# Relation aggregate of a four-layer graph kernel: messages in two float32r parts instead of three bf16 parts, counts cast by halves

## The chip, the cores and the metric

The kernel runs on one core of one Trainium2 chip. The metric is the device time of one execution in microseconds; beside it stands the time of the one execution that the hardware profiler recorded. The engines are named as in the profile: PE is the matrix engine (PEld its weight loads), DVE the vector engine, ACT the scalar engine, POOL GpSimd, SP the engine that issues the transfers.

## What is computed

Four graph layers run in a row on the same 1875 nodes and 60000 edges (`src`, `dst`, sorted by `dst`), each followed by a residual and a layer norm. The change concerns the second layer, which has two relations (edge types):

```python
def _L1_gnn_ref(feat, src, dst, rel, W_rel, b_rel, W_ih, b_ih, b_hh, W1, b1, W2, b2, W3, b3):
    S = feat[src]
    def edge_nn(x, W, b):
        h = jax.nn.relu(x @ W.T + b)
        return jax.nn.relu(h @ W.T + b)
    msgs = jnp.zeros_like(S)
    for r in range(W_rel.shape[0]):
        msgs = jnp.where((rel == r)[:, None], edge_nn(S, W_rel[r], b_rel[r]), msgs)
    agg = jax.ops.segment_sum(msgs, dst, num_segments=n_nodes)
    gates = agg @ W_ih.T + b_ih + b_hh
    ...
```

A message depends on the source node and the relation only. So the kernel computes it once per node and relation, and the sum over edges is a product with a matrix of edge counts: `agg[d] = sum over r, s of count[r][s, d] * message[r][s]`. The third layer (SAGE, two convolutions) sums over all edges in the same way, with the counts of both relations added and a division by the number of edges of each node.

## The kernel before

The nodes are 15 tiles (`NT`, also called `SH`) of 128. The counts lie in `adjacency` (`ADJ`, 128 x 2 x 28320, uint16): for a relation and a source tile `sh`, the 1888 counts (`NW`) of all destinations stand 15 elements apart. Every engine runs its own instruction list, written out by hand and tied together by semaphores; nothing is reordered by a scheduler.

The stages around the change are these.

- **Messages** (PE lines 1733 and 1758, function `messages1` on ACT, `rest` on DVE). For ten groups (two relations, five groups of three node tiles) PE computes the hidden layer into PSUM, ACT applies the ReLU, PE computes three message tiles of 128 x 256 from it. For each of the 30 message tiles ACT writes the ReLU rounded to bf16 (line 691); DVE subtracts it from the PSUM value (1285), writes that remainder as bf16 (1286) and subtracts again into a third bf16 part (1287). PE's message products of a group wait (`m_ev`) until DVE has done the messages of the group before.
- **Relation aggregate** (`aggregate(CH1, R2 * SH, 0)`, PE line 1776). Thirty count chunks, one for a relation and source tile. ACT casts each chunk of 1888 counts to f16 (line 713) into a ring of two; a cast waits until the chunk two before has been used (`chunk_used`). For each chunk PE makes 24 products of 128 x 128 by 128 x 472: three parts, two feature halves (`fo`), four column groups (`j`) of the 1888, all accumulated in the eight PSUM banks.
- **Counts per node** (DVE lines 1318 to 1321), beside the aggregate. Once ACT has cast the last chunk of relation 0, DVE adds the counts of relation 1 to those of relation 0 in place, sums the 15 source tiles into `CNTX`, waits for the end of the aggregate, and copies `CNTX` to `CNTS`.
- **Evacuation** (`agg_evac`, DVE 1314 and 1315, ACT 725): the eight banks go to `XT`, then PE starts the gates (`gates`, line 1796).
- **Weights of the rest of the layer** (SP lines 467 to 470): the loads of `WIH`, `W1s`, `W2s`, `W3s` wait for the last message (`m_ev`).

The two aggregates of the third layer use the same function with one chunk per source tile (15) and with messages in two float32r parts, `halves`: ACT writes the ReLU as float32r, DVE the remainder (1293) as float32r. There the chunk is cast to float32r too, its first 944 columns by ACT (733) and its second 944 by DVE (1378), again in a ring of two. This is the path that the change takes over for the relation aggregate.

A flag (`large`), loaded from the input's counts, selects another path with full float32 messages (`WIDE`); the rows show that the other path ran.

Names: `s["..."]` are the semaphores, `A_...` are offsets (in 4-byte words) into the one large SBUF tensor `arena`, `CW` is 472.

Of the kernel before, what the change touches and what calls it, by code (L numbers as in the profile page):

```python
# [34 lines left out]
D = 256  # L35
# [124 lines left out]
MW = 3 * D // 2  # L160
A_CNT = A_B1 + NT * MW
A_FB = A_WT - RRING * FW
assert A_FB >= A_HB + D and A_OR >= A_X + NT * D
assert A_CNT + NW <= A_CH and A_B1 + R2 * NT * MW <= A_WT and A_B1 + 12 * CN <= A_CNT
# [4 lines left out]
def build(nc, rec, x, xT, edge0, w0, a0l, a0r, cols, hrow, wrel, brow, wih, w1, w2, w3, b3, wp1, bp1, wl1, bl1, wr1, wp2, bp2, wl2, bl2, wr2,  # L169
          wt3, a3l, a3r, out):  # L170
    ctx = ExitStack()
    with ctx:
# [131 lines left out]
        MT = [AR[:, A_B1 + MW * i:A_B1 + MW * (i + 1)] for i in range(R2 * NT)]  # L304
        CNTS = ar(A_CNT, NW)

        def parts(i):
            return [MT[i].bitcast(BF16)[:, D * q:D * (q + 1)] for q in range(3)]

        HALVES = nc.alloc_sbuf_tensor_at("message_halves", [P, 2 * NT * D], F32R, offset=a_at + 4 * A_B1)  # L310
        COUNTS = nc.alloc_sbuf_tensor_at("count_chunks", [P, 2 * NW], F32R, offset=a_at + 4 * A_CH)

        def halves(i):
            return [HALVES[:, D * (2 * i + q):D * (2 * i + q + 1)] for q in range(2)]

        WIDE = [AR[:, A_B1 + D * i:A_B1 + D * (i + 1)] for i in range(R2 * NT)]

        def chunk(at, k, wide):

            if at == CH2 and not wide:  # L320
                return COUNTS[:, k * NW:(k + 1) * NW]
            if wide:
                return AR[:, at[1] + k * NW:at[1] + (k + 1) * NW]
            return AR[:, at[0] + k * NW // 2:at[0] + (k + 1) * NW // 2].bitcast(F16)

        REM = ar(A_REM, D)
        CH1, CH2 = (A_XT + 2 * NP - NW, A_B1 + R2 * NT * D), (A_CH, A_CH)
# [9 lines left out]
        WIH = ar(A_WT + 1024, 2, 3 * D)  # L337
        W1s, W2s, W3s = ar(A_WT + 2560, 2, P), ar(A_WT + 2816, P), ar(A_WT + 2944, D)
# [16 lines left out]
            var_ready std_ready ln_done xt_mm xt_eva xt_evd h_mm h_ev m_mm m_ev chunk_ready chunk_half chunk_used agg_eva  # L355
# [14 lines left out]
        def offsets(engine, step, n, most, table=OFF):  # L370
# [4 lines left out]
                skip_runtime_bounds_check_because="window and tile numbers of the walk stay in range for any sorted edges")[1]  # L375

# [12 lines left out]
        def _(sp):  # L389
# [75 lines left out]
            sp.wait_ge(s["m_ev"], 3 * R2 * NC)  # L465
# [106 lines left out]
        def _(act):  # L572
# [115 lines left out]
            def message(n, bank, wide, exact=False):  # L688

                dst = WIDE[n % (R2 * NT)] if wide else halves(n)[0] if exact else parts(n % (R2 * NT))[0]  # L690
                a.activation(dst, PS[bank][:, 0:D], ACT.Relu).then_inc(s["hi_ready"], 1)

            def messages1(wide):
# [14 lines left out]
                act.wait_ge(s["m_mm"], 3 * R2 * NC)  # L708
                for c in range(R2 * SH):
# [3 lines left out]
                    a.activation(chunk(CH1, c % 2, wide), ADJ[:, r, :].rearrange("p (n s) -> p n s", s=SH)[:, :, sh],  # L713
                                 ACT.Copy).then_inc(s["chunk_ready"], 1)

            with act.If(large < 1):
                messages1(False)
            with act.If(large >= 1):
# [1218 lines left out]
```

## Time and profile before

| what | us |
|---|---|
| median of 3 runs | 1783.98 (1782.76 to 1784.89) |
| the profiled execution | 1781.72 |
| its span, first to last instruction | 1780.0 |
| PE / DVE / ACT / POOL busy | 1422.1 / 1154.4 / 749.8 / 546.0 |
| messages and relation aggregate, from the first hidden product to the first gate product | 1138.2 to 1364.5 |
| in it the relation aggregate's products | 1214.56 to 1360.75 |

The rows quoted further on come from this one profiled execution. Times in them are from the start of its span. In the groups of instructions, "busy, mean ns" are the time in which the group was busy and the mean length of one instruction (matmuls overlap, so the mean times the count is more than the busy time); "idle before" is the time in which the engine did nothing just before such an instruction, with what ended the wait.

### The profile page before, as it was taken

How to read it: one execution, taken by the hardware profiler on the slowest of the kernel's cores; microseconds unless marked ns; L12 is line 12 of the kernel's file. 1: busy time of each engine (PE TensorE's matmuls, PEld its weight loads, DVE VectorE, ACT ScalarE, POOL GpSimd, SP SyncE). 2: the span in 40 equal slices, each digit the busy share in tenths (PEclk: the TensorE clock that was granted, in tenths of full speed). 3: DMA queues.
4: the chain of work that ended last, by engine and by line, in shares of the span. 5: the costliest groups of instructions: out<-in, count | busy, mean ns of one | idle time of the engine just before them, and what ended most of it. 6: DMA issues, size and time to landing. Idle time of an engine off the chain costs nothing.

```text
span 1780.0 us, 21845 instructions
## 1 busy us (share of the span) xinstructions
PE 1422.1 (80%) x5158; PEld 758.0 (43%) x5158; DVE 1154.4 (65%) x2990; ACT 749.8 (42%) x1243; POOL 546.0 (31%) x517
## 2 busy tenths in 40 slices
PE   5897987777777777773499999798999989989840
PEld 2454643411111111112277777454445447758630
DVE  6323543399999999999989988751180443543727
ACT  1333443477777777772000000236774435416022
POOL 0103777777777777771000000000000000000023
PEclk9997555755555555555599999898999979999965
DMA  4534666655555555552098888000000010000023
GB/s 163 167 133 154 210 210 213 211 185 187 185 186 185 179 187 184 186 185 85 25 322 275 266 273 256 1 1 26 1 1 2 0 36 0 2 12 1 1 62 74
DMA packets 84507, 223.90 MB, mean 126 GB/s; under 512 B 18456, under 2 KB 27588, under 8 KB 83908
## 3 DMA queue, kind: packets, MB, share of 16 engines
q1 hardware_dynamic: 60452, 158.01, 25.4%
q0 software_dynamic: 23968, 64.77, 14.0%
q8 instruction: 51, 0.84, 0.2%
q14 instruction: 36, 0.29, 0.1%
HBM read 140.09 MB, written 82.63 MB: 125 GB/s over the span
## 4 chain that ended last, share of the span: by engine, by line
PE 43%; DVE 20%; issue 14%; POOL 6%; DMA 2%; ACT 2%; DVEq 2%; SPq 0%; POOLq 0%
PE bank L1776 14%; PE bank L1711 13%; POOL arena L557 6%; DVE arena L1095 4%; DVE arena L1096 3%; DVE adjacency L1102 3%; PE bank L1796 2%; DVE arena L1137 2%; PE bank L1833 2%; PE bank L1758 2%; PE bank L1733 2%; DMA arena<-feat_table,arena 1%; PE bank L1865 1%; DVEq L372 1%; PE bank L1862 1%
## 5 line engine op out<-in xcount | busy, mean ns | idle before, releaser
L557 POOL DMA_INDIRECT arena<-feat_table,arena x469 | 508.8, 1085 | 240.1 <-issue 227.9
L1650 PE MATMUL bank<-arena 128*128 128x480 f16 x586 | 337.0, 576 | 122.0 <-DVE arena L1096 116.0
L639 ACT ACTIVATE arena<-bank 128x480 uint16<-128x480 f32 x586 | 333.4, 572 | 118.1 <-PE bank L1650 111.6
L565 POOL DMA_INDIRECT arena<-al_table,edge_ends x15 | 14.8, 985 | 917.4 <-DMA al_table<-arena 913.2
L1102 DVE TENSOR_TENSOR adjacency<-adjacency,arena 128x480 uint16 x586 | 235.5, 402 | 9.9 <-DVE arena L1115 6.2
L1650 PEld LDWEIGHTS bank<-arena 128*128 128x128 f16 x586 | 61.0, 104 | 398.3 <-DVE arena L1096 312.0
L1711 PE MATMUL bank<-arena 128*128 x966 | 229.6, 392 | 0.9 <-issue 0.3
L1096 DVE TENSOR_SCALAR arena<-iota,arena 128x480 f16<-128x480 f16 x586 | 199.2, 340 | 0.0
L1711 PEld LDWEIGHTS bank<-arena 128*128 128x128 f32 x966 | 173.4, 190 | 57.3 <-issue 36.4
L1193 DVE TENSOR_TENSOR arena<-arena 128x1024 f32<-128x1024 f32 x118 | 140.1, 1214 | 16.4 <-DMA arena<-edge_rows 14.5
L1776 PE MATMUL bank<-arena 128*128 128x472 f16 x720 | 146.2, 367 | 3.9 <-ACT arena L713 3.9
L1095 DVE TENSOR_SCALAR arena<-iota,arena 128x128 f16<-128x128 f16 x586 | 145.9, 249 | 1.3 <-ACT adjacency L603 1.3
L713 ACT ACTIVATE arena<-adjacency 128x1888 f16<-128x1888 uint16 x30 | 109.0, 3638 | 34.9 <-PE bank L1776 34.9
L1570 PE MATMUL bank<-arena 128*128 128x512 f32 x240 | 108.8, 608 | 5.7 <-ACT arena L588 3.0
L1776 PE MATMUL bank<-count_chunks,message_halves 128*128 128x472 f32 x480 | 103.4, 377 | 2.1 <-DVE message_halves L1293 2.1
L1776 PEld LDWEIGHTS bank<-arena 128*128 128x128 bf16 x720 | 71.1, 99 | 79.3 <-ACT arena L713 4.7
L671 ACT ACT_TABLE_LOAD x2 | 2.6, 1283 | 240.0 <-DVE ln_mean_var L1239 240.0
L1776 PEld LDWEIGHTS bank<-count_chunks,message_halves 128*128 128x128 f32 x480 | 90.0, 188 | 15.5 <-issue 2.9
L1613 PE MATMUL bank<-arena 128*128 x588 | 75.7, 189 | 17.1 <-DVE arena L1052 11.3
L733 ACT ACTIVATE count_chunks<-adjacency 128x944 fp32r<-128x944 uint16 (+1 forms) x30 | 69.9, 2335 | 39.8 <-PE bank L1776 39.8
L1613 PEld LDWEIGHTS bank<-arena 128*128 128x128 f16 x588 | 60.1, 105 | 48.4 <-issue 35.0
L1200 DVE TENSOR_TENSOR arena<-iota,arena 128x1024 f32<-128x1024 f16 (+1 forms) x61 | 73.8, 1210 | 7.0 <-PE bank L1711 6.9
(294 smaller groups left out, 1598.0 us busy)
## 6 DMA issues: line engine op xcount, KB each, us to landing
arena<-edge_rows SPq DMA_DIRECT2D x117, 520.0 KB, 4.7
edge_rows<-arena SPq DMA_DIRECT2D x67, 520.0 KB, 2.9
edge_rows<-arena SPq DMA_DIRECT2D x67, 390.0 KB, 2.6
feat_table<-arena SPq DMA_DIRECT2D x60, 260.0 KB, 2.1
arena<-feat_table,arena POOLq DMA_INDIRECT x469
arena<-in_w SPq DMA_DIRECT2D x1, 2048.0 KB, 9.7
arena<-in_xT SPq DMA_DIRECT2D x1, 1920.0 KB, 18.0
arena<-in_x SPq DMA_DIRECT2D x1, 1792.0 KB
```

What stands on the lines that cost most here:

```text
L557: g.indirect_dma_start(out=PLACE[k][:, t - lo, :], out_offset=None, in_=feat_t, in_offset=bass.IndirectOffsetOnAxis(ap=IE[:, t:t + 1], axi ...
L639: a.activation(EV[st % AS].rearrange("p r k -> p (r k)"), PS[4 + st % 4][:, 0:R2 * KW], ACT.Copy)\
L713: a.activation(chunk(CH1, c % 2, wide), ADJ[:, r, :].rearrange("p (n s) -> p n s", s=SH)[:, :, sh], ACT.Copy).then_inc(s["chunk_ready"], 1)
L1095: v.tensor_scalar(OHS[st % AS], iota128[:, :], lo, None, ALU.is_equal)
L1096: v.tensor_scalar(OHK[st % AS], iota480[:, :], key, None, ALU.is_equal).then_inc(s["a_oh"], 1)
L1102: v.tensor_tensor(dst, dst, EV[st % AS], ALU.add).then_inc(s["a_add"], 1)
L1193: v.tensor_tensor(rows, rows, al, ALU.mult).then_inc(s["r_wgt"], 1)
L1570: ins = mm(PS[c][:, :], XT0[:, k, P * t:P * (t + 1)], W0[:, k, 512 * c:512 * (c + 1)], start=(k == 0), stop=(k == 1))
L1613: ins = mm(PS[4 + g % 2][:, 3 * H * k:3 * H * (k + 1)], KO[g % 3][:, lo:lo + P], ERW[:, bass.ds(offs[k], 3 * H)], start=True, stop=True)
L1650: mm(PS[4 + st % 4][:, 0:R2 * KW], OHS[st % AS], OHK[st % AS], start=True, stop=True).then_inc(s["a_mm"], 1)
L1711: mm(BANKS[:, bass.ds(out_at, D)], OHR[:, (st // RG) % ORING, P * (st % RG):P * (st % RG + 1)], FBf[:, bass.ds(places[st % RK] >> 12, D)], ...
L1776: ins = mm(PS[4 * fo + j][:, 0:CW], m[:, P * fo:P * (fo + 1)], ch[:, CW * j:CW * (j + 1)], start=(c == 0 and q == 0), stop=(c == n - 1 and ...
```

## The change

The relation aggregate gets a function of its own, `aggregate_relations`.

- The message is two float32r parts: ACT writes the ReLU as float32r, DVE one remainder (`low_half` in place of `rest`). The 30 messages take 30 x 512 words in place of 30 x 384 and lie in four places (`halves1`): 22 from `A_M1`, one each at `A_M22` and `A_M23`, and the last six where `XT` is (the transposed input, read for the last time by the hidden products).
- A chunk is cast to float32r in halves of 944 counts (`HW`), 60 in all, in a ring of three (`RING1`, `NRING`). Half `h` waits until half `h - 3` has been used (`half_free`). `cast_on_dve` says who casts: of relation 0 ACT the even and DVE the odd halves; of relation 1 ACT all of the first 11 source tiles, and DVE the odd halves of the last four (halves 53, 55, 57, 59).
- PE makes 8 products per half: two parts, two feature halves, two column groups; 480 in all in place of 720.
- The counts per node: DVE adds the relations once its and ACT's halves of relation 0 are cast, then waits until 19 chunks have been used, because the sum now goes straight to `CNTS`, which lies at `A_CH` among the messages; only after it come DVE's halves of relation 1. The copy from `CNTX` is gone.
- The weights of the rest of the layer move to `A_WIH`, where the first messages lie, and are loaded once 14 chunks have been used.
- The third layer's aggregates keep their work under new names.

```diff
+HW = NW // 2
+NRING, SPLIT1 = 3, SH - 4
...
+A_CNT = A_CH
+A_WIH = A_M1 + 9 * 2 * D
+def cast_on_dve(h):
+    r, sh = h // (2 * SH), h // 2 % SH
+    return h % 2 == 1 and (r == 0 or sh >= SPLIT1)
...
+        def half_free(engine, h):
+            past = h - NRING
+            if past >= 0 and past % 2:
+                engine.wait_ge(s["chunk_used"], past // 2 + 1)
+            elif past >= 0:
+                engine.wait_ge(s["first_half_used"], past // 2 + 1)
...
-            sp.wait_ge(s["m_ev"], 3 * R2 * NC)
+            sp.wait_ge(s["chunk_used"], 14)
...
+            with act.If(large < 1):
+                messages1(False)
+                for h in range(2 * R2 * SH):
+                    if not cast_on_dve(h):
+                        half_free(act, h)
+                        a.activation(RING1[h % NRING], count_half(h), ACT.Copy).then_inc(s["cast_act"], 1)
...
-                link(v.scalar_tensor_tensor(REM, PS[bank][:, 0:D], 0.0, hi, ALU.max, ALU.subtract))
-                link(v.tensor_copy(mid, REM))
-                v.tensor_tensor(lo, REM, mid, ALU.subtract).then_inc(done, 1)
...
             with dve.If(large < 1):
                 for n in range(R2 * NT):
-                    rest(n, n, 4 + n % 3, s["m_ev"], n)
+                    low_half(n, halves1(n), 4 + n % 3, s["m_ev"])
+                for h in range(1, 2 * SH, 2):
+                    half_free(dve, h)
+                    v.tensor_copy(RING1[h % NRING], count_half(h)).then_inc(s["cast_dve"], 1)
+                dve.wait_ge(s["cast_act"], casts_to(2 * SH - 1, False))
+                dve.wait_ge(s["cast_dve"], casts_to(2 * SH - 1, True))
...
-            dve.wait_ge(s["chunk_ready"], SH)
             link(v.tensor_tensor(ADJ[:, 0, :], ADJ[:, 0, :], ADJ[:, 1, :], ALU.add))
-            link(v.tensor_reduce(CNTX, ADJ[:, 0, :].rearrange("p (n s) -> p n s", s=SH), AX.X, ALU.add))
-            dve.wait_ge(s["chunk_used"], R2 * SH)
-            v.tensor_copy(CNTS, CNTX).then_inc(s["cnt_red"], 1)
-            dve.wait_ge(s["cnt_red"], 1)
+            both = ADJ[:, 0, :].rearrange("p (n s) -> p n s", s=SH)
+            with dve.If(large < 1):
+                dve.wait_ge(s["chunk_used"], 19)
+                v.tensor_reduce(CNTS, both, AX.X, ALU.add).then_inc(s["cnt_red"], 2)
+                for h in range(2 * SH, 2 * R2 * SH):
+                    if cast_on_dve(h):
+                        half_free(dve, h)
+                        v.tensor_copy(RING1[h % NRING], count_half(h)).then_inc(s["cast_dve"], 1)
...
+            def add_products(m, ch, j0, start, stop):
+                for fo in range(2):
+                    for j in range(ch.shape[1] // CW):
+                        ins = mm(PS[4 * fo + j0 + j][:, 0:CW], m[:, P * fo:P * (fo + 1)], ch[:, CW * j:CW * (j + 1)], start=start, stop=stop)
+                return ins
...
+                    for h in range(2 * R2 * SH):
+                        c, part = h // 2, h % 2
+                        if cast_on_dve(h):
+                            pe.wait_ge(s["cast_dve"], casts_to(h, True))
+                        else:
+                            pe.wait_ge(s["cast_act"], casts_to(h, False))
+                        hi, lo = halves1(c)
+                        add_products(hi, RING1[h % NRING], 2 * part, c == 0, False)
+                        add_products(lo, RING1[h % NRING], 2 * part, False, c == R2 * SH - 1)\
+                            .then_inc(s["chunk_used"] if part else s["first_half_used"], 1)
```

Two places show how the instructions now stand. DVE before, from the last message to the evacuation of the aggregate (`[waits ...]` names the semaphores an instruction waits for; line numbers are those of the kernel before):

```order
L1285 SCALAR_TENSOR_TENSOR arena<-bank,arena 128x256 [waits m_ev,hi_ready]
L1286 CAST arena<-arena 128x256 [waits dve_link]
L1287 TENSOR_TENSOR arena<-arena 128x256 [waits dve_link]
...
L1318 TENSOR_TENSOR adjacency<-adjacency 128x28320 [waits chunk_ready]
L1319 TENSOR_REDUCE arena<-adjacency 128x1888 [waits dve_link]
L1321 COPY arena<-arena 128x1888 [waits chunk_used,dve_link]
L1314 COPY arena<-bank 128x472 [waits chunk_used,cnt_red]
```

DVE of the change at the same place (line numbers of the changed kernel; `count_half_0` and `count_halves_1_2` are the three places of the ring, `last_messages` the last six messages; the number behind a name is the buffer's):

```order
L1327 SCALAR_TENSOR_TENSOR last_messages_54<-bank,last_messages_54 128x256 [waits hi_ready] x6
L1339 CAST count_halves_1_2_56<-adjacency 128x944
L1339 CAST count_half_0_55<-adjacency 128x944 [waits first_half_used]
L1339 CAST count_halves_1_2_56<-adjacency 128x944 [waits first_half_used] x2
...
L1334 UNCONDITIONAL_BRANCH [waits cast_dve,cast_act]
...
L1354 TENSOR_TENSOR adjacency<-adjacency 128x28320
L1356 COMPARE_AND_BRANCH [waits dve_link]
L1358 TENSOR_REDUCE arena<-adjacency 128x1888 [waits chunk_used]
L1362 CAST count_halves_1_2_56<-adjacency 128x944 [waits first_half_used] x2
L1362 CAST count_half_0_55<-adjacency 128x944 [waits first_half_used]
L1362 CAST count_halves_1_2_56<-adjacency 128x944 [waits first_half_used]
```

Fifteen casts now stand ahead of the addition, and four stand behind the sum over source tiles (halves 53, 55, 57, 59), which itself waits for a used chunk; the copy is gone.

ACT before, from the last messages on:

```order
L691 ACTIVATE arena<-bank 128x256 [waits m_mm] x6
L713 ACTIVATE arena<-adjacency 128x1888 [waits m_mm]
L713 ACTIVATE arena<-adjacency 128x1888
L713 ACTIVATE arena<-adjacency 128x1888 [waits chunk_used] x28
```

ACT of the change at the same place, with the change from relation 0 to relation 1 at the end of the piece:

```order
L731 ACTIVATE last_messages_54<-bank 128x256 [waits m_mm] x6
L755 ACTIVATE count_half_0_55<-adjacency 128x944 [waits m_mm]
L755 ACTIVATE count_halves_1_2_56<-adjacency 128x944
L755 ACTIVATE count_halves_1_2_56<-adjacency 128x944 [waits chunk_used]
...
L755 ACTIVATE count_half_0_55<-adjacency 128x944 [waits chunk_used]
L755 ACTIVATE count_halves_1_2_56<-adjacency 128x944 [waits first_half_used]
L755 ACTIVATE count_halves_1_2_56<-adjacency 128x944 [waits chunk_used]
L755 ACTIVATE count_half_0_55<-adjacency 128x944 [waits first_half_used]
```

Thirty whole chunks have become 41 halves: every other half of relation 0, then one half after the other.

## Rows read from the trace of the kernel before

**Rows 1.** The page's first lines: span, and PE's busy time.
```profile
span 1780.0 us, 21845 instructions
...
PE 1422.1 (80%) x5158; PEld 758.0 (43%) x5158; DVE 1154.4 (65%) x2990; ACT 749.8 (42%) x1243; POOL 546.0 (31%) x517
```
**Rows 2.** The chain that ended last, 1100 to 1780: start us, us, what.
```profile
1151.70 2.58 PE bank L1733 x8
...
1211.04 3.48 ACT arena L713
1214.56 146.19 PE bank L1776 x720
1360.85 1.16 DVE arena L1321
1362.03 2.32 DVE arena L1314 x4
1364.52 10.73 PE bank L1796 x24
...
1378.43 7.85 PE bank L1796 x24
```
**Rows 3.** Groups of instructions by line and shape, 1136 to 1378.
```profile
L1776 PEld LDWEIGHTS bank<-arena 128*128 128x128 bf16 x720 | 71.1, 99 | 79.3 <-ACT arena L713 4.7 <-issue 3.3
```
**Rows 4.** The same view, 1447 to 1535: the third layer's first aggregate.
```profile
L1776 PE MATMUL bank<-count_chunks,message_halves 128*128 128x472 f32 x240 | 51.7, 377 | 1.0 <-DVE message_halves L1293 1.0
L1776 PEld LDWEIGHTS bank<-count_chunks,message_halves 128*128 128x128 f32 x240 | 45.0, 188 | 7.8 <-issue 1.4
L733 ACT ACTIVATE count_chunks<-adjacency 128x944 fp32r<-128x944 uint16 x13 | 27.8, 2135 | 19.9 <-PE bank L1776 19.9
L1378 DVE CAST count_chunks<-adjacency 128x944 fp32r<-128x944 uint16 x13 | 15.1, 1158 | 31.2 <-PE bank L1776 31.2
```
**Rows 5.** Timeline, start of the aggregate: start us, us, instruction [idle before <-releaser].
```profile
1203.39 0.42 DVE L1285 SCALAR_TENSOR_TENSOR arena<-bank,arena 128x256 f32<-128x256 f32 x1
1204.18 0.42 DVE L1287 TENSOR_TENSOR arena<-arena 128x256 bf16<-128x256 f32 x1
1204.75 0.26 PE L1756 MATMUL bank<-arena,ones 3*128 3x256 bf16 x1 [1.91 <-DVE arena L1287]
1204.94 1.13 PE L1758 MATMUL bank<-arena 128*128 128x256 f32 x4
1208.54 2.08 PE L1758 MATMUL bank<-arena 128*128 128x256 f32 x4
1210.93 7.05 ACT L713 ACTIVATE arena<-adjacency 128x1888 f16<-128x1888 uint16 x2
```
**Rows 6.** Stretches: PE, PEld, DVE, ACT, POOL busy (instructions), PEclk, DMA share, GB/s.
```profile
1203.00:1206.00 3.00, 1.25 (x5) 0.77 (x5) 1.43 (x4) 0.27 (x1) 0.00 (x0) 1.00 0.00 0
1208.00:1210.50 2.50, 2.50 (x6) 1.27 (x5) 1.15 (x3) 0.38 (x1) 0.00 (x0) 0.50 0.00 0
1217.00:1219.90 2.90, 2.90 (x9) 1.11 (x8) 0.00 (x0) 0.99 (x1) 0.00 (x0) 0.50 0.01 5
1219.90:1225.00 5.10, 5.10 (x27) 2.50 (x26) 0.00 (x0) 2.84 (x1) 0.00 (x0) 1.00 0.00 0
1364.50:1370.00 5.50, 5.48 (x9) 3.08 (x10) 0.00 (x0) 0.58 (x1) 0.00 (x0) 0.50 0.00 0
1478.00:1482.00 4.00, 3.29 (x15) 2.93 (x16) 0.42 (x1) 0.08 (x1) 0.00 (x0) 1.00 0.00 0
```
**Rows 7.** Timeline, ACT in the relation aggregate: beside nothing, beside DVE's sum.
```profile
1255.62 3.64 ACT L713 ACTIVATE arena<-adjacency 128x1888 f16<-128x1888 uint16 x1 [1.15 <-PE bank L1776]
1260.40 3.63 ACT L713 ACTIVATE arena<-adjacency 128x1888 f16<-128x1888 uint16 x1 [1.14 <-PE bank L1776]
...
1303.42 3.64 ACT L713 ACTIVATE arena<-adjacency 128x1888 f16<-128x1888 uint16 x1 [1.12 <-PE bank L1776]
```
**Rows 8.** Timeline, ACT in the third layer's aggregate: two casts with their waits.
```profile
1489.29 2.13 ACT L733 ACTIVATE count_chunks<-adjacency 128x944 fp32r<-128x944 uint16 x1 [1.31 <-PE bank L1776]
...
1496.14 2.13 ACT L733 ACTIVATE count_chunks<-adjacency 128x944 fp32r<-128x944 uint16 x1 [1.26 <-PE bank L1776]
```
**Rows 9.** Timeline, DVE in the relation aggregate: addition and sum.
```profile
1283.18 14.91 DVE L1318 TENSOR_TENSOR adjacency<-adjacency 128x28320 uint16<-128x28320 uint16 x1 [70.90 <-ACT arena L713]
1298.13 29.65 DVE L1319 TENSOR_REDUCE arena<-adjacency 128x1888 f32<-128x28320 uint16 x1
```
**Rows 10.** Timeline, SP: the first of the four weight loads.
```profile
1212.31 0.38 SPq L467 DMA_DIRECT2D arena<-in_wih  x1
```

More of the change, by code:

```diff
@@ L712, in messages1 @@
                         act.wait_ge(s["chunk_used"], c - 1)
[L713 to L718, printed above, removed]
-                messages1(True)
+                    a.activation(chunk(CH1, c % 2, True), ADJ[:, r, :].rearrange("p (n s) -> p n s", s=SH)[:, :, sh],
+                                 ACT.Copy).then_inc(s["cast_act"], 1)
             def agg_evac(dst, total):
@@ L1307, in _ @@
                     no_rest(n, s["m_ev"])
[L1308 removed]
+                dve.wait_ge(s["cast_act"], SH)
             def agg_evac(dst, total):
@@ L1761, in _ @@
             pe.wait_ge(s["m_ev"], 3 * R2 * NC)
-            def aggregate(at, n, first):
-                def products(wide):
-                    for c in range(n):
-                        pe.wait_ge(s["chunk_ready"], first + c + 1)
-                        if at == CH2 and c >= 2:
-                            pe.wait_ge(s["chunk_half"], (first // SH - R2) * (SH - 2) + c - 1)
-                        ch = chunk(at, c % 2, wide)
-                        ms = [WIDE[c]] if wide else halves(c) if at == CH2 else parts(c)
-                        for q, m in enumerate(ms):
-                            for fo in range(2):
-                                for j in range(4):
-                                    ins = mm(PS[4 * fo + j][:, 0:CW], m[:, P * fo:P * (fo + 1)], ch[:, CW * j:CW * (j + 1)],
-                                             start=(c == 0 and q == 0), stop=(c == n - 1 and q == len(ms) - 1))
+            def add_products(m, ch, j0, start, stop):
[3 more added lines that the diff above has]
+                return ins
@@ new lines, in aggregate, with chunks @@
+            def aggregate(u):
+                def chunks(wide):
+                    for c in range(SH):
+                        pe.wait_ge(s["chunk_ready"], SH * u + c + 1)
+                        if c >= 2:
+                            pe.wait_ge(s["chunk_half"], u * (SH - 2) + c - 1)
+                        ch = chunk(CH2, c % 2, wide)
+                        if wide:
+                            ins = add_products(WIDE[c], ch, 0, c == 0, c == SH - 1)
+                        else:
+                            hi, lo = halves(c)
+                            add_products(hi, ch, 0, c == 0, False)
+                            ins = add_products(lo, ch, 0, False, c == SH - 1)
```

83 lines of the change are left out of this document (51 added, 32 removed).

## The prediction

> **What bounds the kernel now.** I read the page first [rows 1]: PE is busy 80% of the span, but that is an average over stages. The chain that ended last [rows 2] shows the stage of the change by itself: 720 products of line 1776 follow one another for 146.19 us with nothing else between them, so the relation aggregate is bound by PE. Ahead of it the chain runs over ACT's first cast, behind it over DVE's copy (1.16 us) and its evacuation (2.32 us). Whatever shortens PE's work here shortens the kernel until another engine is later than PE. So I need PE's pace, the pace of the casts, and DVE's long instructions.
>
> **PE's pace.** ACT's casts in the steady part start 4.78 us apart [rows 7], one per 24 products: 199.2 ns each. 720 x 0.1992 = 143.4 us. The other 2.8 us of the 146.19 are the clock: from 1214.56 to 1219.9 the granted clock was 0.50, the 1.2 GHz level, then 1.00 [rows 6]; half of 5.3 us is 2.7 us lost. The new products are those of the third layer's aggregate, same shape and type. There ACT's casts start 3.425 us apart over 16 products (6.85 us for two chunks, [rows 8]): 214 ns each, 1.715 us for a half of 8. 60 halves: 102.9 us. Were PE never to wait, the stage would shrink by 40 us.
>
> The float32r weights load slower: 188 ns on average against 99 ns for bf16 [rows 3, 4]. The 15 ns by which a product is slower may come from that. The Trainium skill ("TensorE: Matmul & The Clock Gate", Weight-path perf modes) says that fast weight load is on only where the type isn't FP32; the 188 against 99 agrees. It speaks against the change; by it alone, with the longer load fully in the open (89 ns x 480), the sum would be some 43 us longer, but the third layer's aggregate already runs at 214 ns with these loads, so I keep 214.
>
> **The casts.** A half on ACT took 2.13 us, beside DVE's cast that starts at the same instant, a half on DVE 1.16 us [rows 4]. Alone, a half on ACT is not in the trace. From below: half of a whole chunk, 3.63 / 2 = 1.81 us [rows 7]; from above 2.13. I take 1.9, nearer to the whole chunk, which also ran alone. Two casts in a row took 7.05 us [rows 5] against 2 x 3.63, so one follows the other some 0.15 us before the length says: a pace of 1.75 (1.65 to 2.0).
>
> Let t = 0 be PE's first product, at full clock. In relation 0, half h may be cast from the end of half h-3 and is needed when h-1 ends, 3.43 us later. ACT needs 0.2 us (the semaphore) + 2.1 + 0.1 = 2.4, DVE 1.5: no wait. In relation 1 ACT casts 22 halves in a row, from h = 30. That one is ready at 28 x 1.715 + 0.2 + 2.0 = 50.2 and needed at 51.5. At 1.75 ACT loses 0.035 a half on PE: never late. At 2.0 it is late by 5 us at h = 52.
>
> **DVE is the one that is late.** Its last cast of relation 0 (half 29) starts when half 26 ends, 46.5, and ends at 47.7. The addition takes 14.9 us [rows 9]: 62.7. The sum waits for 19 used chunks, 38 halves: 38 x 1.715 + 0.2 = 65.4; the addition is covered by 2.7 us. The sum takes 29.65 us [rows 9]: 95.05. Half 53 stands behind it in DVE's queue: + 1.16 + 0.1 = 96.3. PE wants it at 53 x 1.715 = 90.9. **PE stands still for about 5 us at half 53**, or for 1 us if ACT's pace is 2.0, with the same end. Then 7 halves remain, 12.0 us: 108.3. The other halves of DVE and ACT fit in the ring (3.43 us against 1.5 and 2.4).
>
> The clock: I keep the 2.7 us at the start: 111.0. The stall is a second occasion. After the 3.8 us without products before 1364.5 the granted clock was 0.50 until 1370 [rows 6], also 5.5 us, 2.7 lost; after the gap of 1.0 before the third layer's aggregate it stayed 1.00 [rows 4, 6]. A stall of 5 us resembles the first, so I add 2.7: **113.7 us for the aggregate, 32.5 less than 146.2**.
>
> **The edges of the stage.**
> - PE's first product waited for a whole chunk: last message product until 1210.62, cast from 1210.93, product at 1214.56 [rows 2, 5]. A half is enough now (1.9 + 0.1): 1212.9, **1.6 us** less. Half 1 on DVE (one short instruction for the last message, then 1.16) is ready then too.
> - DVE's work on a message falls from three instructions to one. PE sees it once, at the last group, where nothing else covers: it waited 1.91 us [rows 5] for DVE, whose last message ran from 1203.39 to 1204.60. Now it ends after the first instruction, 1203.81: **0.8 us** less. The other nine groups are covered by the next hidden products (2.58 us, [rows 2]).
> - The copy to CNTS goes from the chain: 1.16 us, **1.2** with its semaphore [rows 2]. The evacuation (2.32) stays.
> - The weight loads: SP issued them from 1212.31 [rows 10]; now after 14 chunks (28 halves, 48 us into the stage), with some 60 us until the gates. Nothing stands behind them on SP but the bias rows that wait for the aggregate's end as before. Cost nothing; were the cover gone, the gates would wait for the landing. More instructions and waits on ACT (41 for 30): inside the 1.75. Storage moves cost nothing.
>
> **Sum.** 32.5 + 1.6 + 0.8 + 1.2 = 36.1 us less. On the profiled execution: 1781.7 - 36.1 = 1745.6. The median of the runs is 2.3 us above that execution, so 1784.0 - 36.1 = 1747.9; I say **1748**. From no change I could tell 0.2%, 3.6 us.
>
> **Unknown terms.** Below: no clock price at the stall (-2.7), none at the start (-2.7), and the fall of the clock at 1206 [rows 6] avoided with the shorter gap there (two message tiles at 2.08 in place of 1.13, [rows 5], -1.9). Above: DVE's sum beside an ACT that never pauses (before, it paused 1.14 of 4.78 us; up to +1), or the clock low for all 12 us after the stall (+9.3).
>
> **Rivals.**
> - *The stall doesn't cost clock* (27%). For: the chunk before ran at full speed; if ACT's pace is near 2.0, the waiting is spread over many halves and the gap at 53 is 1 us. 1748 - 2.7 = 1745. The Trainium skill (same page, The HAM clock gate) says that the level follows recent activity and that the array is slowed after idleness; which gap suffices only the rows above bear on: 1.0 us no, 3.8 yes.
> - *ACT is the bound of relation 1* (6%). If its pace passes 2.03 (from 50.2 + 22p + 1.7 > 96.3), half 53 waits for half 52 and each 0.1 us adds 2.2 us. At 2.2 this is +4: 1752. Against: no row of ACT shows a half above 2.2.
> - *Clock low longer after the stall* (8%): up to 1757.
> - *A change of weights costs* (4%). A weight tile now serves two products, before four. If each change cost the whole load, 4 more changes per chunk, 30 x 4 x 0.188 = 22.6 us on PE: 125.5 + 2.7 = 128.2, with the stall absorbed: 1784 - 18.0 - 3.6 = 1762. Against: there is one load per product already [rows 4].
> - *The loads come into the open* (3%), the other side. If every product waited for its own load, 197 + 188 = 385 ns, the stage would be 480 x 0.385 + 2.7 = 187.5 us: 1784 + 41.3 - 3.6 = 1822. It becomes slower than before from (143.4 + 3.6) / 480 = 306 ns a product. Against: 214 ns in rows of the same shape; the waits at every half instead of every chunk are all that could break the overlap.
> - *Not what it says*: if the flag chose the full float32 path, nothing of this would run; the rows of before show the bf16 and f16 shapes on the same input. Under 1%.
>
> **How the numbers follow.** Forecast 50%, no clock price 27, clock low longer 8, ACT the bound 6, change of weights 4, loads in the open 3, the rest 2 (some gain lost elsewhere, about no change). The range reaches down to 1741 (the three clock terms) and up to 1757 (low clock to the end): it leaves out the last three cases and a piece of the others. Faster 0.95, same 0.02, slower 0.03.
>
> **What would show it.** 480 products of 8 per half, 214 ns apart; ACT's halves of relation 1 at 1.8 to 2.0 us; the sum of 29.7 us starting 68 us after PE's first product (65.4 + 2.7); one idle of PE of 1 to 5 us in front of half 53, released by DVE's cast; granted clock 0.50 behind it; no copy between aggregate and evacuation; PE idle 2.3 us before the first product. Wrong if products are farther apart than 220 ns, if PE waits for ACT's halves in relation 0, or if the sum isn't followed by a stall.

## The result and the profile after

The changed kernel takes 1737.16 us (median of 4 runs, 1733.44 to 1739.31) against 1783.37 us before (4 runs, 1781.29 to 1784.89): ratio 0.9745, 95% interval 0.9718 to 0.9772, or 46 us less. I had said 1748, with 1741 to 1757. The direction and the place are right; the gain is 10 us larger than forecast, and the measured time lies 4 us below the range.

The profiled execution of the changed kernel took 1739.31 us, its span 1737.6. First its page (head and PE's busy time, which answer to [rows 1]):

```profile
span 1737.6 us, 21308 instructions
...
PE 1378.4 (79%) x4918; PEld 774.2 (45%) x4918; DVE 1153.8 (66%) x2948; ACT 722.7 (42%) x1254; POOL 545.3 (31%) x517
```

The chain that ended last in the stage (start us, us, what), which answers to [rows 2]:

```profile
1209.95 1.81 ACT count_half L755
1211.81 59.66 PE bank L1813 x272
...
1275.49 3.97 PE bank L1813 x16
...
1279.56 29.65 DVE arena L1358
1309.21 0.93 DVE count_halves L1362
...
1310.18 12.29 PE bank L1813 x56
...
1322.49 2.32 DVE arena L1351 x4
...
1324.99 7.98 PE bank L1866 x24
```

DVE's sum (line 1358) and the cast of half 53 behind it (line 1362) stand in the chain between two runs of products, as forecast, and 56 products, seven halves, are left behind it; the copy ahead of the evacuation is gone. The first 24 gate products took 7.98 us where they took 10.73 before. Timelines: PE at the last message tiles, at the start of the aggregate and at half 53; then DVE from its addition to the casts of halves 53 and 55.

```profile
1205.67 0.26 PE L1802 MATMUL bank<-arena,ones 3*128 3x256 bf16 x1 [1.02 <-DVE last_messages L1327]
1211.81 3.37 PE L1813 MATMUL bank<-count_half,first_messages 128*128 128x472 f32 x8 [2.27 <-ACT count_half L755]
...
1310.18 1.98 PE L1813 MATMUL bank<-count_halves,last_messages 128*128 128x472 f32 x8 [1.64 <-DVE count_halves L1362]
```
```profile
1261.17 14.91 DVE L1354 TENSOR_TENSOR adjacency<-adjacency 128x28320 uint16<-128x28320 uint16 x1 [0.52 <-DVE count_halves L1339]
1279.56 29.65 DVE L1358 TENSOR_REDUCE arena<-adjacency 128x1888 f32<-128x28320 uint16 x1 [3.47 <-PE bank L1813]
1309.13 2.01 DVE L1362 CAST count_halves<-adjacency 128x944 fp32r<-128x944 uint16 x2
```

The stretches that answer to [rows 6] (columns as there; the granted clock is the number ahead of the last two) are, in this order, the last messages, the start of the aggregate, the products behind the stall, and the gates.

```profile
1205.50:1209.50 4.00, 3.83 (x15) 2.30 (x15) 0.87 (x3) 0.77 (x2) 0.00 (x0) 1.00 0.00 0
1211.80:1215.00 3.20, 3.19 (x8) 2.74 (x9) 0.00 (x0) 1.78 (x1) 0.00 (x0) 0.52 0.00 0
...
1310.20:1313.00 2.80, 2.80 (x13) 2.48 (x14) 0.94 (x1) 0.80 (x1) 0.00 (x0) 1.00 0.00 0
...
1325.00:1330.00 5.00, 5.00 (x16) 3.01 (x17) 0.00 (x0) 2.47 (x4) 0.00 (x0) 1.00 0.01 3
```

Only one of the four is low, the start of the aggregate, for 3.2 us instead of 5.3. Before, the last messages and the gates were low too.

From such timelines I made one sheet for every profile: the time from the first hidden product to the last message product, then each gap and block of products. The stage runs from the first hidden product to the second group of gate products; in it, behind the first 24 gate products, 30 products of one column stand that take 3.2 us in every profile and have no column. A block of gates is counted to the start of the next product, so 10.73 and 7.98 us above are 10.6 and 7.8 here. "Ahead" and "behind" are what lies before and after the stage. All in us.

| kernel | messages | gap | aggregate | gap | 24 gate products | stage | ahead | behind |
|---|---|---|---|---|---|---|---|---|
| before | 72.6 | 3.9 | 146.2 | 3.8 | 10.6 | 240.3 | 1138.0 | 401.7 |
| change | 69.7 | 2.3 | 110.6 | 2.5 | 7.8 | 196.2 | 1139.8 | 401.6 |

The stage gives 44.1 us: 2.9 + 1.7 + 35.5 + 1.2 + 2.7. The rest of the program gives back 1.7, nearly all of it ahead of the stage, where nothing was changed.

### The profile page after: what moved, and what is told of

It is laid out like the page before. It is cut to its first block, busy times and chain, and to the rows that moved or that the text cites. A ratio compares the mean times of both kernels' runs of the same rounds, so it can differ in the third digit from the quotient of the medians.

```text
span 1737.6 us, 21308 instructions
## 1 busy us (share of the span) xinstructions
PE 1378.4 (79%) x4918; PEld 774.2 (45%) x4918; DVE 1153.8 (66%) x2948; ACT 722.7 (42%) x1254; POOL 545.3 (31%) x517
## 4 chain that ended last, share of the span: by engine, by line
PE 43%; DVE 22%; issue 10%; POOL 6%; ACT 5%; DMA 3%; DVEq 2%; SPq 0%; POOLq 0%
PE bank L1757 13%; PE bank L1813 11%; POOL arena L597 6%; DVE arena L1139 4%; ACT arena L679 3%; DVE arena L1140 3%; PE bank L1696 3%; DVE adjacency L1146 3%; PE bank L1866 2%; PE bank L1903 2%; DVE arena L1181 2%; PE bank L1804 2%; DMA arena<-feat_table,arena 2%; DVE arena L1358 2%; PE bank L1779 2%
## 5 line engine op out<-in xcount | busy, mean ns | idle before, releaser
L1146 DVE TENSOR_TENSOR adjacency<-adjacency,arena 128x480 uint16 x586 | 252.0, 430 | 10.2 <-DVE arena L1159 6.2
L1140 DVE TENSOR_SCALAR arena<-iota,arena 128x480 f16<-128x480 f16 x586 | 216.2, 369 | 0.0
L1757 PEld LDWEIGHTS bank<-arena 128*128 128x128 f32 x966 | 175.6, 191 | 54.9 <-issue 32.9
L1139 DVE TENSOR_SCALAR arena<-iota,arena 128x128 f16<-128x128 f16 x586 | 162.9, 278 | 0.9 <-ACT adjacency L643 0.9
L628 ACT ACTIVATE arena<-bank 128x512 f32<-128x512 f32 x60 | 35.8, 597 | 99.9 <-PE bank L1616 96.2
L1645 PE MATMUL bank<-adjacency,ident 128*128 128x512 f16 x128 | 66.2, 616 | 12.6 <-ACT arena L655 9.7
L1616 PEld LDWEIGHTS bank<-arena 128*128 128x128 f32 x240 | 46.8, 199 | 62.0 <-issue 54.8
```

The costliest lines, as they stand in the source:

```text
L1139: v.tensor_scalar(OHS[st % AS], iota128[:, :], lo, None, ALU.is_equal)
L1140: v.tensor_scalar(OHK[st % AS], iota480[:, :], key, None, ALU.is_equal).then_inc(s["a_oh"], 1)
L1146: v.tensor_tensor(dst, dst, EV[st % AS], ALU.add).then_inc(s["a_add"], 1)
L1616: ins = mm(PS[c][:, :], XT0[:, k, P * t:P * (t + 1)], W0[:, k, 512 * c:512 * (c + 1)], start=(k == 0), stop=(k == 1))
L1757: mm(BANKS[:, bass.ds(out_at, D)], OHR[:, (st // RG) % ORING, P * (st % RG):P * (st % RG + 1)], FBf[:, bass.ds(places[st % RK] >> 12, D)], ...
```

## The experiments

Fifteen more runs were made: twelve edited kernels, the changed kernel twice more and the kernel before once more. The sheet has a profile of each, with the gap in front of half 53, the time from the first gate product to the third layer's first product ("gates"), and the median time with the number of runs in brackets. Executions of the changed kernel lie up to 6 us apart, so the time of a single run settles nothing smaller; the readings below rest on the blocks.

| kernel | messages | aggregate | gap at 53 | gap | 24 gate products | stage | gates | behind | time |
|---|---|---|---|---|---|---|---|---|---|
| before | 72.6 | 146.2 | | 3.8 | 10.6 | 240.3 | 90.9 | 401.7 | 1783.37 (4) |
| e_before_again | 71.2 | 145.9 | | 3.8 | 10.4 | 238.4 | 91.0 | 397.9 | 1776.91 (1) |
| change | 69.7 | 110.6 | 1.6 | 2.5 | 7.8 | 196.2 | 86.4 | 401.6 | 1737.16 (4) |
| e_again | 69.8 | 110.7 | 1.7 | 2.5 | 7.8 | 196.4 | 85.7 | 397.9 | 1735.51 (5) |
| e_after_third | 69.8 | 110.6 | 1.5 | 2.5 | 7.8 | 196.2 | 88.5 | 397.3 | 1734.50 (1) |
| e_copy_back | 69.8 | 110.7 | 1.5 | 3.7 | 9.5 | 199.1 | 98.8 | 408.8 | 1748.31 (1) |
| e_three_ops | 73.1 | 110.9 | 1.7 | 2.5 | 7.8 | 199.8 | 86.5 | 401.5 | 1741.08 (1) |
| e_longer_stall | 69.7 | 115.2 | 4.5 | 2.5 | 7.8 | 200.7 | 91.6 | 399.9 | 1741.67 (1) |
| e_no_sum | 69.8 | 108.8 | 0 | 2.5 | 9.5 | 196.1 | 90.3 | 401.1 | 1739.37 (1) |
| e_no_sum_split | 69.7 | 106.0 | 0 | 2.5 | 9.5 | 193.2 | 92.0 | 404.6 | 1740.08 (1) |
| e_all_act | 68.8 | 109.2 | 0 | 2.5 | 9.3 | 195.4 | 93.7 | 403.6 | 1737.65 (1) |
| e_ring_two | 68.6 | 123.8 | 0 | 2.5 | 7.8 | 208.2 | 90.4 | 404.5 | 1752.63 (1) |
| e_sum_early | 69.7 | 108.8 | 0 | 2.5 | 9.5 | 196.0 | 90.3 | 397.7 | 1735.13 (4) |
| e_sum_in_pieces | 69.8 | 105.9 | 0 | 2.5 | 9.5 | 193.2 | 87.9 | 401.4 | 1735.82 (5) |
| e_early_gates | 69.7 | 110.6 | 1.7 | 0.8 | 7.8 | 194.4 | 91.0 | 399.2 | 1735.24 (4) |
| e_pieces_early_gates | 69.9 | 106.1 | 0 | 0.8 | 7.8 | 190.0 | 86.3 | 401.2 | 1734.70 (5) |
| e_pieces_gap | 69.4 | 106.1 | 1.4 | 2.6 | 9.4 | 193.0 | 93.9 | 404.2 | 1735.19 (1) |

**The changed kernel and the kernel before, again** (e_again, e_after_third, e_before_again; no edit).

> The changed kernel once more, unchanged, to see how far single executions scatter. Theory A (the stage gives a fixed gain, the rest scatters): the stage from the first hidden product to the second group of gate products takes 196.1 us again within 0.5, the aggregate 110.7, and times lie between 1733 and 1740 with a gain of 42 to 48 us over the kernel before; what varies lies ahead of 1140 us. Theory B (the clock falls in the stage in some executions, not in others): the aggregate or the gates differ by 1 to 3 us from the first profile.

> The changed kernel a third time. Theory A (a matter of the moment): aggregate 110.7, and gates at another length than the 86.4 and 85.8 us of the first two profiles, up to 99. Theory B (the shorter gap in front of the gates keeps the clock up): 85.5 to 86.5 us again, first 24 gate products in 7.8.

> The kernel before, once more, to see whether the time behind the aggregate varies from one execution to the next. Theory A (the granted clock in the gates is a matter of the moment): aggregate 146.2 again, but 86 to 99 us from the first gate product to the third layer's first product, where the first profile had 90.9. Theory B (it is fixed by the kernel): 90.9 within 0.5.

e_again: 1735.51 us (5 runs, 1733.08 to 1738.33), before beside it 1783.08 (9 runs, 1775.42 to 1788.81), ratio 0.974, interval 0.9714 to 0.9766. The stage is the same in three profiles of the changed kernel within 0.2 us: theory A on the stage. But what varies does not lie ahead of 1140 us, as theory A had it: the three profiles differ by 1.4 us there and by 4.3 us behind the stage (397.3 to 401.6). e_after_third is between its theories: the first 24 gate products took 7.8 us again, as B had it, and all gates 88.5 us after 86.4 and 85.7, as A had it. The kernel before repeats its gates (90.9, 91.0), which is theory B of e_before_again, while its stage moved by 1.9 us. The clock did that: in the second profile it rose sooner at the first hidden products (1.0 us less for the first eight), the last messages lost 0.4 us less and the aggregate 0.3. So a part of what the clock costs belongs to the kernel and a part to the execution.

**The copy put back.**

> The changed kernel with a copy of 1888 elements on the vector engine put back between the aggregate and its evacuation, as before. Theory A (the evacuation's gap had cost clock): PE's gap in front of the gates grows from 2.5 to 3.7 us and the first 24 gate products take 10.7 us in place of 8.0 at a granted clock of 0.50 in their first 5 us; together 3.9 us. Theory B (the copy cost only itself): gap 3.7 us, products 8.0 us; together 1.2 us.

```diff
+            dve.wait_ge(s["chunk_used"], R2 * SH)
+            link(v.tensor_copy(AR[:, A_B1:A_B1 + NW], CNTS))
             agg_evac(XT, R2 * SH)
```

The copied counts are not used. The gap grew by 1.2 us as said, the first 24 gate products went from 7.8 to 9.5 us, and the clock was low in a part of them:

```profile
1325.00:1329.00 4.00, 3.95 (x9) 2.22 (x10) 0.00 (x0) 0.58 (x1) 0.00 (x0) 0.68 0.02 4
1329.00:1334.70 5.70, 5.70 (x20) 3.40 (x18) 0.00 (x0) 2.33 (x4) 0.00 (x0) 0.93 0.00 0
```

Together 2.9 us: theory A with 1.7 in place of 2.7 us of clock. The clock fell in four later groups of gates too, each time behind two waits of 0.67 us that left it up in the three profiles of the changed kernel. All gates took 98.8 us against 86.4, which no theory had, and this one execution 1748.31 us. Whether the copy or the execution did that, one profile can't tell.

**Three instructions a message again.**

> The changed kernel with two more vector instructions for each of the 30 messages (their results are not used), so that a message takes three instructions again. Theory A (the 1.9 us gap at the last group pulled the clock down): the gap grows from 1.0 to 1.9 us, the granted clock falls at the last messages (the last two tiles at 2.0 us in place of 1.1), and the first products of the aggregate stay low for longer than 3.2 us; together 0.9 + 1.9 + about 1.2 = 4 us. Theory B (the gap cost only itself): 0.9 us. The nine other groups cost nothing in both.

```diff
-                    low_half(n, halves1(n), 4 + n % 3, s["m_ev"])
...
+                    link(v.scalar_tensor_tensor(lo, PS[4 + n % 3][:, 0:D], 0.0, hi, ALU.max, ALU.subtract))
+                    link(v.tensor_copy(REM.bitcast(BF16)[:, 0:D], PS[4 + n % 3][:, 0:D]))
+                    v.tensor_tensor(REM.bitcast(BF16)[:, D:2 * D], PS[4 + n % 3][:, 0:D], REM.bitcast(BF16)[:, 0:D], ALU.subtract).then_inc(s["m_ev"], 1)
...
```

```profile
1205.16 0.26 PE L1808 MATMUL bank<-arena,ones 3*128 3x256 bf16 x1 [2.22 <-DVE arena L1340]
...
1206.73 2.07 PE L1810 MATMUL bank<-arena 128*128 128x256 f32 x4
...
1209.06 2.08 PE L1810 MATMUL bank<-arena 128*128 128x256 f32 x4
```

The gap became 2.2 us, 0.3 more than before (the second of the three instructions reads PSUM here and took 0.42 us, before 0.29), and the last two tiles took 2.07 and 2.08 us where the changed kernel has 1.13: messages 3.4 us longer, 1.2 by the gap and 2.2 by the clock. Theory A for the messages; of the 1.2 us that it had for the start of the aggregate only 0.2 came.

**A longer stall.**

> The changed kernel with a sum over 2640 elements (2.8 us, result not used) on the vector engine in front of its cast of half 53. PE's gap there should grow from 1.6 to about 4.4 us. Theory A (a gap of about 4 us lowers the clock): granted clock 0.50 behind it for 3 to 5.5 us, the aggregate takes 110.7 + 2.8 + 1.5 to 2.7 = 115 to 116.2 us. Theory B (after a long stretch of dense products the clock stays): 113.5 us, granted clock 1.00 throughout.

```diff
+                        if h == 53:
+                            v.tensor_reduce(REM[:, 0:176], both[:, 0:176, :], AX.X, ALU.add)
                         v.tensor_copy(RING1[h % NRING], count_half(h)).then_inc(s["cast_dve"], 1)
```

```profile
1312.63 2.90 PE L1815 MATMUL bank<-count_halves,last_messages 128*128 128x472 f32 x8 [4.46 <-DVE count_halves L1364]
```
```profile
1312.60:1316.60 4.00, 3.97 (x12) 3.39 (x13) 0.96 (x1) 1.03 (x1) 0.00 (x0) 0.60 0.00 0
```

115.2 us: 2.8 for the longer gap and 1.7 for the clock, theory A at its lower end. So a stall of 4.5 us does lower the clock here; the stall of 1.6 us that the change has does not.

**What bounds the aggregate: sum left out, casts moved, ring shortened.**

> The changed kernel without the sum over source tiles: the counts per node are set to 1 in its place, so the third layer's mean is left out. Theory A (DVE is late only by its sum, ACT's pace does the rest): the gap in front of half 53 goes (1.6 us), the aggregate takes 109.0 us, and ACT's halves of relation 1 still start 1.94 us apart. Theory B (the sum also slows ACT's casts beside it): ACT's pace falls to 1.8 us and the aggregate takes 106 to 107 us.

> The same without the sum, and DVE casts the odd halves of the last ten source tiles of relation 1 in place of the last four. Theory A (ACT's pace of 1.94 us against PE's 1.71 costs the rest): the aggregate takes 104 to 105 us (60 halves at 1.711 = 102.7, 1.5 for the low clock at the start, under 1 for ACT's first halves of relation 1). Theory B (something in PE itself, the semaphore wait at every half or the weight loads): products beyond 1.75 us a half, 107 us or more.

> The changed kernel with all halves of relation 1 on ACT. Theory A (ACT's pace bounds relation 1, DVE's four halves hardly help because they come late): no gap at half 53, PE 1.94 us a half to the end (1.9 once the sum is over); half 53 starts at 98.2 us instead of 98.4 us after the first product and the seven halves left take 7 x 1.94 = 13.6 in place of 12.1: the aggregate takes 110 to 112 us. Theory B (DVE's halves are needed): 114 us or more.

> The changed kernel with a ring of two halves in place of three. Theory (a half may then be cast only from the end of the half two before, 1.71 us ahead of its use): in relation 0 a pair of halves takes 0.2 + 2.05 + 0.1 + 1.71 = 4.1 us in place of 3.42, 10 us more over 15 pairs; in relation 1 about 2.03 us a half in place of 1.94, 1 to 2 us more: the aggregate takes 121 to 123 us. Rival (PE's order of loads and waits hides it, or casts overlap more than the rows say): under 114 us.

```diff
-                v.tensor_reduce(CNTS, both, AX.X, ALU.add).then_inc(s["cnt_red"], 2)
+                v.memset(CNTS, 1.0).then_inc(s["cnt_red"], 2)
```
```diff
-NRING, SPLIT1 = 3, SH - 4
+NRING, SPLIT1 = 3, SH - 10
+NRING, SPLIT1 = 3, SH
+NRING, SPLIT1 = 2, SH - 4
```

The first edit is that of the two kernels without the sum: all counts per node are 1 in them, so the third layer's mean is left out. Of the second, the first new line goes with it in e_no_sum_split, the second is e_all_act and the third e_ring_two, each alone.

Without the sum the aggregate takes 108.8 us (109.0 expected) and ACT's pace doesn't change:

```profile
1281.90 4.10 ACT L755 ACTIVATE count_halves<-adjacency 128x944 fp32r<-128x944 uint16 x2
1285.77 2.14 ACT L755 ACTIVATE count_half<-adjacency 128x944 fp32r<-128x944 uint16 x1
1287.68 4.09 ACT L755 ACTIVATE count_halves<-adjacency 128x944 fp32r<-128x944 uint16 x2
```

Three halves in 5.78 us, 1.93 each, as beside the sum: theory A. With DVE helping from half 41 on it takes 106.0, 1 us above what I had allowed: ACT is alone for the first eleven halves of relation 1, and the halves 33 to 41 still start 1.94 us apart. All halves on ACT: 109.2, under the 110 to 112 expected; but in this execution the start of the aggregate ran at full clock, worth 1.5 us, and with that it is 110.7, the changed kernel's own time. So DVE's four halves as placed seem to gain nothing, as far as one profile with a correction shows. The ring of two costs 13 us (15 with the same correction for its start), a little above the 121 to 123 us expected: in relation 0 PE waits 0.4 us at every second half, in relation 1 the halves start 2.08 us apart, so the third place is needed.

**Two versions with a shorter aggregate.**

> The changed kernel with CNTS two message places lower, so that DVE's sum waits for 17 used chunks in place of 19. Theory A (DVE's chain makes half 53 late): the sum starts when the addition ends, 64.3 us after PE's first product in place of 67.8, half 53 is ready before PE wants it, the gap of 1.6 us goes and the aggregate takes 109.0 us, as without any sum (108.75). Theory B (ACT's pace would be the bound by more than the gap): under 0.5 us gained.

> A version meant to beat both kernels: CNTS as in the early sum; DVE takes half 39 and all odd halves from 47 on in place of 53 on, and its sum runs in nine pieces, 944 nodes behind half 39 and 118 (the last 236) behind each later half. Theory A (DVE's one long instruction and ACT's pace are what is left above PE's own 102.7 + 1.5): the aggregate takes 105 to 106.5 us, without a gap above 0.5 us. Theory B (the pieces delay DVE's halves, each now behind 1.9 us of sum, as soon as PE catches up): 108 us or more with gaps at odd halves. The time: 1736 less 4 to 6 us, within the scatter of the gates' clock.

```diff
-A_CNT = A_CH
+A_CNT = A_WIH + 2176
...
-                dve.wait_ge(s["chunk_used"], 19)
+                dve.wait_ge(s["chunk_used"], 17)
```
```diff
-    return h % 2 == 1 and (r == 0 or sh >= SPLIT1)
+    return h % 2 == 1 and (r == 0 or sh >= SPLIT1 or h == FIRST1)
...
+                def sum_nodes(n):
+                    ins = v.tensor_reduce(CNTS[:, done[0]:done[0] + n], both[:, done[0]:done[0] + n, :], AX.X, ALU.add)
...
                         v.tensor_copy(RING1[h % NRING], count_half(h)).then_inc(s["cast_dve"], 1)
+                        if h == FIRST1:
+                            dve.wait_ge(s["chunk_used"], 17)
+                        sum_nodes(8 * PIECE if h == FIRST1 else 2 * PIECE if h == 2 * R2 * SH - 1 else PIECE)
```

Both aggregates came out as theory A had them, 108.8 and 105.9 us. The second has `FIRST1` 39, `SPLIT1` SH - 7 and `PIECE` 118, and three things at once: the early sum (1.9 us by e_sum_early), the sum in pieces, and four more halves on DVE; the two last share the other 2.8 us and weren't tried apart. And yet the stages are 196.0 and 193.2, where 194.3 and 191.5 were due: the first 24 gate products went from 7.8 to 9.5 us, with this at their start in the second:

```profile
1319.70:1323.70 4.00, 3.95 (x7) 2.21 (x8) 0.00 (x0) 1.37 (x2) 0.00 (x0) 0.57 0.02 4
```

The medians, 1735.13 (4 runs) and 1735.82 us (5 runs), ratios 0.9743 (0.971 to 0.9775) and 0.9748 (0.9721 to 0.9775), can't be told from the changed kernel's.

**The gap in front of the gates.** Every variant without a wait in relation 1 of the aggregate had the slower gates (e_no_sum, e_no_sum_split, e_all_act and these two), so I shortened the gap, and put the stall back.

> The changed kernel; PE starts the gates once the first bank of each half is evacuated, and takes each further bank when it is free, in place of waiting for all eight. The gap in front of the gates should fall from 2.5 to 0.9 us. Theory A (the gap lowers the clock, or just doesn't): first 24 gate products in 7.8 us as in the three profiles of the changed kernel; stage 196.2 - 1.6 = 194.6 us. Theory B (the clock depends on more than the gap): 9.5 us, stage 196.3.

> The sum in pieces with the early gates. The aggregate takes 105.9 us again, the gap 0.9 us. Theory A (in a kernel without a stall in the aggregate it is the gap of 2.5 us that lowers the clock): first 24 gate products in 7.8 in place of 9.5 us; stage 193.2 - 1.6 - 1.7 = 189.9 us, 6 us less than the changed kernel, its time 1729 to 1732 with the scatter of the rest. Theory B (where the clock falls is a matter of the moment): 9.5 us, stage 191.6.

> The sum in pieces with 3.8 us of unused sum in front of DVE's half 53, so that PE stands still there for about 1.8 us as the changed kernel does. Theory A (the short stall some 12 us ahead of the gap is why the changed kernel's gates ran at full clock): first 24 gate products in 7.8 us in place of 9.5, so that the stall pays for itself: aggregate 107.7, stage 193.3 us. Theory B (chance, or a matter of when the aggregate ends): 9.5 us, stage 195.0.

```diff
-                    v.tensor_copy(dst[:, 0, CW * j:CW * (j + 1)], PS[j][:, 0:CW])
+                    v.tensor_copy(dst[:, 0, CW * j:CW * (j + 1)], PS[j][:, 0:CW]).then_inc(s["m_ev"], 1)
...
-            pe.wait_ge(s["agg_evd"], 1)
-            pe.wait_ge(s["agg_eva"], 4)
...
+                    elif j < 4:
+                        pe.wait_ge(s["m_ev"], 3 * R2 * NC + j + 1)
+                    if c == 0:
+                        pe.wait_ge(s["agg_eva"], max(1, j - 3))
```

The full waits now stand behind the first group of gates. The gap fell to 0.8 us, and with the sum in pieces the gates returned to 7.8 us:

```profile
1316.00:1320.00 4.00, 3.81 (x12) 2.38 (x13) 1.85 (x6) 3.71 (x7) 0.00 (x0) 1.00 0.03 7
```

Its stage of 190.0 us is the shortest, 6.2 us under the change (189.9 expected). With the changed kernel's own aggregate the early gates gave 1.8 us in the stage; all gates took 91.0 us there, 4.6 more than in the change's first profile, so the stage's gain didn't reach the end.

e_pieces_gap has the pieces, the full waits ahead of the gates, and 3.8 us of unused sum in front of half 53:

```diff
                         half_free(dve, h)
+                        if h == 53:
+                            v.tensor_reduce(REM[:, 0:236], both[:, 0:236, :], AX.X, ALU.add)
```

PE stood still for 1.4 us there, and the gates stayed at 9.4 us: theory B, the stall didn't pay for itself in this one profile. Its aggregate, 106.1, again started at full clock; with the 1.5 us it is 107.6, as expected.

Times: e_early_gates 1735.24 us (4 runs), ratio 0.9732 (0.9708 to 0.9756); e_pieces_early_gates 1734.70 us (5 runs, 1730.15 to 1736.35), ratio 0.9719 (0.97 to 0.9737). The last is the lowest ratio of all, but its interval overlaps the changed kernel's. The 6 us of the stage are shown in the trace, a shorter total isn't.

## Why the prediction was wrong, step by step

The step that failed is the price of the clock. I added 2.7 us for a fall behind the stall, which didn't come, and I left the low clock as it was behind the three waits that the change shortens, where it shrank or went: 1.2 us at the start, 2.0 at the last messages, 2.7 in the gates. The rest of the sum holds within 1 us.

- **PE's pace** (214 ns): right. The halves start 1.71 us apart in relation 0 and 1.72 at the end, about 102.7 us for 60. The weight loads are 188 ns on average again (197 for the products that ran partly at the low clock), in the open nowhere. The two rivals on weight loads are out; the third layer's aggregate was the right place to read the price.
- **ACT's half** (1.9 us, pace 1.75): mis-sized. It took 2.0 to 2.3 us, also without a DVE cast beside it; only the first two took 1.90 us (PE idle) and 1.93 (PE's first products at the low clock). The pace was 2.0 us beside the addition and 1.93 after: at the upper end of my 1.65 to 2.0. PE lost some 4.5 us by it in short waits until half 52, and 1.6 us at once at half 53. (For a pace of 2.0 my own terms give 0.4 us there, not the 1 us that I wrote: half 52 ends at 95.9, half 53 is cast at 96.3.)
- **ACT is the bound** (rival, 6%): it didn't come, but it was close. With DVE's sum out of the way the aggregate takes 108.8 us, so DVE's end lay only 1.9 us behind ACT's. Of what is left above PE's own 102.7 and the clock's 1.5 us, ACT's pace is the larger part, and the forecast doesn't have it.
- **DVE is late at half 53**: right, and by luck so close. The sum started 67.75 us after the first product (68.1 said), took 29.65, and PE waited for the cast behind it. e_no_sum and e_sum_early took this wait away: 1.9 us. Two errors cancel in the 67.75: the clock at the start cost 1.2 us less, and ACT made PE late before the 19th chunk was used, with halves 33 to 38 starting 1.97 us apart in place of 1.71, 1.3 us in all. So the end does depend on ACT's pace, by the wait for 19 chunks, which I had denied.
- **The clock at the stall** (+2.7): wrong, and this was the choice between forecast and first rival (27%). I compared the stall of 5 us with the gap of 3.8. With ACT at 2.0 the stall was 1.6, and the rival's reason, waiting spread over many halves, was the one that came. e_longer_stall shows that the term exists, 1.7 us, from a stall of 4.5 us.
- **The clock at the start** (2.7 kept): 1.5 measured, since the low stretch was 3.2 us long.
- **The clock at the last messages**: named only as a bound (-1.9); it came in full, 2.0 us, and e_three_ops, one profile, brings it back. The shorter gap was in my own sum, and with it a reason to expect no fall; I should have taken it into the forecast.
- **The clock in the gates**: missing. The gap there fell from 3.8 to 2.5 us by the copy that I did count, and the 2.7 us of low clock behind it [rows 6], which I quoted for another purpose, went too. e_copy_back returns 1.7 of them. But the shorter gap alone doesn't explain it: six other kernels lost 1.5 to 1.7 us behind the same gap. Why the change's gates ran at full clock stays open.
- **Edges**: 1.6, 0.8 and 1.2 us forecast, 1.7, 0.9 and 1.2 measured. The weight loads from memory cost nothing.

Of the stage's 44.1 us I had 36.1: the missing 8.0 are 2.7 (stall), 1.2 (start), 2.0 (messages), 2.7 (gates), and 0.2 at the edges, less 0.8 by which the sum over source tiles, and with it the rest of the aggregate, came later than I had it (the 1.3 us above, less 0.5 by PE's slightly faster pace and a shorter semaphore). That puts the profiled execution at 1745.6 - 8.0 = 1737.6, and it took 1739.3, the rest of the program being 1.7 longer. The other 4.4 us between 1748 and 1737 are my step from one execution to the median: the profile of before lay 2.3 us below its median, that of the change 2.1 above. The program scatters by 6 us with the change and by 13 us before (1775.4 to 1788.8), so a range for a median of four needed some us for that alone; mine had none.

## What to carry to other kernels

When a change shortens waits of PE, price each low-clock stretch behind such a wait as a term of its own, with a range: here the waits gave 3.8 us directly and 5.9 us more went with the low clock (2.0, 1.2, 2.7). Where a long instruction stands ahead of short ones that others wait for, start it earlier and cut it into pieces that fit between them: with four more halves on DVE this took 4.7 us from the aggregate. Then look at what comes behind the next wait: with the aggregate shortened, the first gates lost 1.7 us of clock until the gap ahead of them was shortened too, and a shorter total wasn't shown in either case.

## What the runs showed of the hardware

The same gap of 2.5 us ahead of the gates (2.6 in e_pieces_gap) left the clock up in six profiles (three of them of one kernel) and lowered it in six of other kernels, for 1.5 to 1.7 us each. A gap of 3.7 or 3.8 us lowered it in all three cases, one of 0.8 us in neither of two. Ahead of the last messages 1.9 and 2.2 us lowered it in all three profiles that have them, and 1.0 us in none. The length of one wait isn't all: in six profiles (e_longer_stall, e_no_sum_split, e_all_act, e_ring_two, e_early_gates, e_pieces_gap) the clock fell within 1.3 us behind the 30 products of one column, with no wait of PE above 0.2 us in the 4 us before. All their gates took 90.4 to 93.9 us, those of the change 85.7 to 88.5.

The Trainium skill ("TensorE: Matmul & The Clock Gate", The HAM clock gate) says that the chip looks at activity by a clock of its own that doesn't start with the kernel; the traces agree in so far as e_all_act, e_ring_two and e_pieces_gap had full clock at the start of the aggregate behind the same 2.3 us gap that cost the others 1.5 us, with the same instructions up to there. In these three and in e_before_again the clock had also risen sooner at the first hidden products: the first eight took 3.1 to 3.9 us up to the next product, and 4.2 to 4.4 in the other thirteen profiles. So the outcome behind a gap belongs in part to the execution. The three profiles of the change are all of the common kind, and don't show what its gates do in the other. What decides within a kernel stays open: the stall was tried as a cause in one profile, e_pieces_gap, which was of the other kind, and the gates stayed slow. The rival that the moment of the gap on the chip's clock decides, and not its length or the stall, is untested; no run moved the gap alone.

A cast of 944 strided counts on ACT took 1.90 us while PE was idle and 2.0 to 2.3 us while PE ran float32r products at full clock. Why wasn't tried.
